# Stack rows element first, context and key/value weights loaded twice side by side, and a new order of DVE's work in a cross-attention and expert layer

## The chip, the cores and the metric

The kernel runs on one NeuronCore of a Trainium2 chip. The metric is the device time of one execution in microseconds (us), the median of several runs.

## What is computed

The input x is 8 sequences of 128 tokens with 256 features, the context 8 x 128 x 64. The reference, cut to what matters:

```python
# cross attention, 16 heads of 16 elements
qp = layernorm(x) @ Wq.T                       # 256 x 256
k, v = split(ctx @ Wkv_expand.T)               # Wkv_expand: 512 x 64
scores = einsum('bhqd,bhkd->bhqk', qh, kh) / 4, masked causally
out = softmax(scores) @ vh
x = x + out @ Wout.T
# experts: 8 of them, 2 chosen for each token
logits = xf @ (gate_weight + 2 * gate_B @ gate_A).T
gup = xf @ gate_up_proj[e] + lora;  h = silu(gates) * h
y = sum over the two chosen experts of weight * (h @ down[e] + lora)
x = x + y
```

All is float32, with tolerances that make the kernel split float32 values into parts that TensorE multiplies at speed.

## The kernel before, in words

The kernel is written with one instruction stream for each engine: SP (all DMA issues), POOL, ACT, DVE and TensorE (PE). Semaphores named in the code order them; within an engine everything runs in the order written, so one wait holds up everything behind it on that engine.

**Projections.** The batches form two groups of four (`GT = 4`). For each group DVE takes the statistics of x (`group_stats`, L552 and L553), POOL turns variances into 1/sqrt (`normaliser`, L301 and L302), DVE normalises into xhat (`normalise_group`, L557), TensorE transposes xhat (`x_T`, L867) and the context (`context_T`). The context and the key/value weights have 64 columns; their transposed blocks are wanted twice, in partitions 0 to 63 and 64 to 127 (the second copy is multiplied by the low part). `transpose_twice` (L840) makes the copies by a transposition (L842) and a plain product with the identity (L843). Then `kv_proj` and `q_proj` give k, v and q.

**Parts.** Scores are computed in bfloat16 from three parts of q and of k. ACT copies the first part from the bank (`first_part`), DVE subtracts it (`remainder`, L591), ACT makes the second part (`second_part`), and the third is a subtraction by POOL for k (`k_third_parts`, L296) and by DVE for q (`q_third_part`, L597). In POOL's stream `normaliser(0, GT, NT)`, which waits for the statistics of all eight batches, stands at L325, ahead of `k_third_parts(0)` at L327. SP writes the parts of a group to DRAM (`write_parts`, L225), the k set and then the q set, each set in three issues.

**Stacks.** For each batch b, `load_stack(b)` (L228 to L240) reads six stacked blocks of 16 rows back, in three loads for k_st and three for q_st, by `SLOTS = ((0, 0, 3), (1, 3, 2), (2, 5, 1))`: q part 0 three times against k parts 0, 1, 2; q part 1 twice against k parts 0, 1; q part 2 once against k part 0. A row is 16 heads x 128 tokens in bfloat16, 4 KB. One product over the 96 rows then gives all six part products of a head's scores (`s_chunk`, L976 and L980, a batch in four chunks). Both tensors have three buffers.

**Attention.** DVE takes the row maxima (`max_chunk`, L654) and splits them into three parts (`max_parts`, L669 to L673), TensorE transposes these (`max_T`, L1009), ACT copies them (`mT_copy`, L450) and SP loads them as three more rows of q_st (`load_max`, L244), so that the transposed scores (`sT_chunk`, L995) come out with the maximum subtracted. ACT takes the exponential (L456), POOL masks (L356), TensorE multiplies with v (L1168). Between the chunks TensorE, DVE, ACT and POOL also prepare the expert weights (`lora_product`, `merge`, `merge_high`, `merge_low`). The order of all of this is written out by hand in the loop over b from L1094 (TensorE) and L761 (DVE).

**SP's order** after the input loads: write k parts and q parts of group 0, `load_stack` of batches 0, 1, 2, `load_max(0)`, write k parts of group 1, `load_max(1)`, write q parts of group 1, then in turn `load_stack(3)`, `load_max(2)`, `load_stack(4)` and so on.

**Experts.** From about 111 us the expert products take over (L836 and L1060), 16 steps (two groups, eight experts).

Of the kernel before, what the change touches and what calls it, by code (L numbers as in the profile page):

```python
# [12 lines left out]
def cross_attention_moe_kernel(nc, x, ctx_kv, Wq, Wkv, Wout, gate_w, gate_A, gate_B,  # L13
# [11 lines left out]
    P = 128  # L25
    B, S, H = x.shape
    L = ctx_kv.shape[2]
    HD = 16
    NH = H // HD
# [3 lines left out]
    HC = H // P  # L33
    NT = B
    GT = 4
# [21 lines left out]
    ctx = ExitStack()  # L57
    with ctx:
        def sb(name, shape, dt=F32):
            return ctx.enter_context(nc.sbuf_tensor(name, shape, dt))  # L60
# [3 lines left out]


        x_sb = sb("x_sb", [P, NT, H])
        ctx_sb = sb("ctx_sb", [P, NT, L])
        raw = sb("raw", [P, HC * H + 4 * HC * L])
        wq_raw = raw[:, 0:HC * H].rearrange("p (c n) -> p c n", c=HC)
        wkv_raw = raw[:, HC * H:HC * H + 2 * HC * L].rearrange("p (c l) -> p c l", c=2 * HC)  # L70
        wo_raw = sb("wo_raw", [P, HC, H])
        gw_raw = sb("gw_raw", [E, H])
        ga_raw = sb("ga_raw", [R, H])
# [32 lines left out]
        ident = sb("ident", [P, P])  # L106
# [51 lines left out]
        qk_dram = nc.dram_tensor("qk_parts", (2, NT, 3, HD, NH // HC, HC, P), BF16, kind="Internal").ap()  # L158
# [27 lines left out]
        def S_(name):  # L186
            if name not in made:
                made[name] = sem(name)
            return made[name]
# [10 lines left out]
        @block.sync  # L200
        def _(sp):
            sp.dma_start(x_sb[:, 0:GT, :], x_v[:, 0:GT, :]).then_inc(ld["x0"], 16)
            sp.dma_start(wkv_raw, wkv_v).then_inc(ld["wkv"], 16)
            sp.dma_start(ctx_sb[:, :, :], ctx_v).then_inc(ld["ctx"], 16)
            sp.dma_start(wq_raw, Wq.rearrange("(c p) h -> p c h", p=P)).then_inc(ld["wq"], 16)
            sp.dma_start(x_sb[:, GT:NT, :], x_v[:, GT:NT, :]).then_inc(ld["x1"], 16)
            sp.dma_start(upA_raw[:, :], gup_A.rearrange("e r h -> (e r) h")).then_inc(ld["upA"], 16)
# [20 lines left out]
            def load_stack(b):  # L228
                if b >= 3:
                    sp.wait_ge(S_("sT_ready"), NC * (b - 2))  # L230
                sp.wait_ge(S_("k_written"), 16 * 3 * (b // GT + 1))
                for _, first, count in SLOTS:
                    src = qk_dram[1, b, 0:count].rearrange("s d h c n -> (s d) (h c n)")
                    dst = k_st[first * HD:(first + count) * HD, b % 3, :, :].rearrange("p h n -> p (h n)")
                    sp.dma_start(dst, src).then_inc(stack_loaded[b % 3], 16)  # L235
                sp.wait_ge(S_("q_written"), 16 * 3 * (b // GT + 1))
                for part, first, count in SLOTS:
                    src = qk_dram[0, b, part].rearrange("d h c n -> d (h c n)")[None].to_broadcast([count, HD, NH * P])
                    dst = q_st[first * HD:(first + count) * HD, b % 3, :, :].rearrange("p h n -> p (h n)")
                    sp.dma_start(dst, src).then_inc(stack_loaded[b % 3], 16)  # L240

# [297 lines left out]
        def _(dve):  # L539
# [20 lines left out]
            def normalise_group(g):  # L560
                dve.wait_ge(S_("rstd1_ready"), g + 1)
                if g:
                    dve.wait_ge(S_("x_T"), HC * g)
                for t in range(GT):
                    normalise(0, g * GT + t, xhat[:, t, :], "xhat_ready")
# [4 lines left out]
            def group_stats(g):  # L570
                dve.wait_ge(ld[f"x{g}"], 16)
                for t in range(g * GT, (g + 1) * GT):
                    norm_stats(0, t, "mv1_ready")
# [21 lines left out]
            def q_third_part(g, i):  # L595
                dve.wait_ge(S_("part2"), 4 * g + i + 1)
                dve.tensor_tensor(QK_PART(ORDER[i], 2), rest[:, i, :].rearrange("p (t n) -> p t n", t=GT),  # L597
                                  QK_PART(ORDER[i], 1), ALU.subtract).then_inc(S_("q_part3"), 1)
# [26 lines left out]
                        bank[2][:, ic * H + a * P:ic * H + (a + 1) * P].rearrange("p (h d) -> p h d", d=HD),  # L625
                        wqT_hi[:, ic, cols].rearrange("p (d h) -> p h d", d=HD), "wq_lo_ready", SCALE)
            input_lows(0)
            group_stats(1)
            remainder(0, 0)
            remainder(0, 1)  # L630
            normalise_group(1)
            remainder(0, 2)
            remainder(0, 3)
            q_third_part(0, 2)
            q_third_part(0, 3)
            dve.wait_ge(S_("lora_T"), 1)
            dve.tensor_scalar(loraBT[:, :, :].rearrange("p a n -> p (a n)"), bank[3][:, :], LORA, None, ALU.mult)\
                .then_inc(S_("lora_ready"), 1)
# [193 lines left out]
        def _(pe):  # L832
# [4 lines left out]
                if done:  # L837
                    last.then_inc(S_(done), 1)

            def transpose_twice(out_, in_):  # L840

                pe.transpose(out_[0:L, :], in_, ident[:, :])  # L842
                return pe.matmul(out_[L:P, :], in_, ident[:, :], start=True, stop=True)  # L843

            pe.wait_ge(S_("ident_made"), 1)

            pe.wait_ge(ld["wkv"], 16)
            for oc in range(2 * HC):
                last = transpose_twice(bank[3][:, oc * P:(oc + 1) * P], wkv_raw[:, oc, :])
            last.then_inc(S_("wkv_T"), 1)  # L850

            def context_T(g):
                if g == 0:
                    pe.wait_ge(ld["ctx"], 16)
                else:
                    pe.wait_ge(S_("v_ready"), 2 * g)
                for t in range(GT):
                    last = transpose_twice(bank[4][:, t * P:(t + 1) * P], ctx_sb[:, g * GT + t, :])
                last.then_inc(S_("c_T"), 1)

            def x_T(g):
# [351 lines left out]
```

## Time and profile before

| | us |
|---|---|
| median of 3 runs (206.45 to 208.89) | 207.55 |
| span of the profiled execution | 204.6 |
| TensorE busy | 166.9 (82%) |
| DVE busy | 132.7 (65%) |
| ACT busy | 79.9 (39%) |
| POOL busy | 60.0 (29%) |
| hardware DMA queue, share of 16 engines | 34.4% |

The profiled execution has a span, from its first to its last instruction, and no separate time; the span is 2.95 us under the median of the runs shown. The busy times overlap. A row of the timeline names the start, the time taken and the engine of a run of equal instructions; in brackets stand the idle time before it and what ended it. The granted clock is that of TensorE, 1.00 is 2.4 GHz and 0.50 is 1.2 GHz. A DMA share is the mean busy share of the core's 16 DMA engines.

### The profile page before, as it was taken

The page shows a single profiled execution, that of the slowest core. Times are in us where ns is not written, and L with a number is a line of the kernel's source. Part 1 is how long each engine was busy: PE and PEld are TensorE (multiplying, and loading weights), DVE is VectorE, ACT ScalarE, POOL GpSimd, SP SyncE. Part 2 cuts the span into 40 slices and gives each one's busy share as a digit, 9 for nine tenths or more (in the row PEclk, how much of TensorE's full clock was granted, in tenths as well). Part 3 has the DMA queues.
Part 4 walks back from the last instruction along what each step waited for, and adds up shares of the span by engine and source line. Part 5 has one row for each costly group of instructions (what it writes and reads, how often), then busy time and mean ns, then how long its engine had stood idle before and what let it go on. Part 6 is the DMA issues. An engine that isn't in the chain of part 4 may idle for free.

```text
span 204.6 us, 3326 instructions
## 1 busy us (share of the span) xinstructions
PE 166.9 (82%) x1238; PEld 131.4 (64%) x1245; DVE 132.7 (65%) x273; ACT 79.9 (39%) x151; POOL 60.0 (29%) x87
## 2 busy tenths in 40 slices
PE   0999297976888048887695979989999999999993
PEld 0458155854566037765574757778888888888882
DVE  3399955465887137888897878469639746545452
ACT  2136423750285014453553355742434623322230
POOL 7651900130055403764858383311000000000000
PEclk9999855799699757999999999999999999999999
DMA  6989466641618610314230000083000047300003
GB/s 170 232 215 386 139 179 167 157 120 61 186 33 222 133 68 33 84 69 123 58 112 32 3 4 0 26 245 145 0 3 0 0 164 254 103 0 0 5 0 103
DMA packets 23073, 20.63 MB, mean 101 GB/s; under 512 B 7400, under 2 KB 19456, under 8 KB 23056
## 3 DMA queue, kind: packets, MB, share of 16 engines
q1 hardware_dynamic: 23056, 20.41, 34.4%
q8 instruction: 10, 0.16, 0.3%
q14 instruction: 7, 0.06, 0.1%
HBM read 16.08 MB, written 4.23 MB: 99 GB/s over the span
## 4 chain that ended last, share of the span: by engine, by line
PE 42%; DMA 25%; DVE 18%; SPq 7%; ACT 3%; issue 3%; POOL 1%; DVEq 0%; ACTq 0%
PE bank L836 24%; DMA q_st<-qk_parts 17%; PE bank L1060 10%; DVE xhat L557 4%; DMA qk_parts<-parts 3%; SPq L240 3%; DMA q_st<-mT 2%; DVE m_sb L654 2%; DMA raw<-in_L_xattn_Wkv_expand 2%; SPq L235 2%; PE bank L980 1%; DVE stats L552 1%; PE bank L843 1%; SPq L244 1%; PE bank L867 1%
## 5 line engine op out<-in xcount | busy, mean ns | idle before, releaser
L654 DVE TENSOR_REDUCE m_sb<-bank 128x4 f32<-128x512 f32 x32 | 21.1, 681 | 14.0 <-PE bank L980 13.9
L356 POOL TENSOR_SCALAR_AFFINE_SELECT probsT<-probsT 128x512 f32<-128x512 f32 x32 | 20.1, 647 | 22.4 <-ACT probsT L456 22.4
L836 PE MATMUL bank<-xT_hi,up_hi 128*128 128x512 f32 x64 | 25.6, 400 | 0.0
L836 PE MATMUL bank<-xT_hi,up_lo 128*128 128x512 f32 x64 | 25.4, 397 | 0.0
L836 PE MATMUL bank<-xT_lo,up_hi 128*128 128x512 f32 x64 | 25.1, 393 | 0.0
L456 ACT ACTIVATE probsT<-bank 128x512 f32<-128x512 f32 x32 | 17.9, 590 | 17.9 <-PE bank L995 17.9
L980 PE MATMUL bank<-k_st,q_st 96*128 96x128 bf16 x128 | 13.8, 235 | 12.7 <-DMA q_st<-qk_parts 12.6
L378 ACT ACTIVATE h_hi<-up_w 128x512 fp32r<-128x512 f32 x16 | 10.1, 632 | 30.7 <-DVE up_w L726 26.1
L719 DVE TENSOR_TENSOR up_w<-bank,up_w 128x512 f32<-128x512 f32 x16 | 11.0, 688 | 14.2 <-PE bank L836 13.0
L1060 PE MATMUL bank<-dn_hi,h_hi 128*128 128x256 f32 x64 | 18.3, 285 | 0.1
L1060 PE MATMUL bank<-dn_lo,h_hi 128*128 128x256 f32 x64 | 18.2, 284 | 0.0
L1060 PE MATMUL bank<-dn_hi,h_lo 128*128 128x256 f32 x64 | 17.8, 279 | 0.0
L660 DVE TENSOR_TENSOR h_lo<-up_w,h_hi 128x512 fp32r<-128x512 f32 x16 | 11.0, 690 | 9.0 <-ACT h_hi L378 9.0
L976 PEld LDWEIGHTS bank<-causal,ident_b 128*128 128x128 bf16 x32 | 3.4, 105 | 18.2 <-DMA q_st<-qk_parts 13.8
L980 PEld LDWEIGHTS bank<-k_st,q_st 96*128 96x128 bf16 x128 | 11.1, 107 | 5.4 <-issue 1.9
L301 POOL TENSOR_SCALAR var_eps<-mv 128x1 f32<-128x1 f32 (+1 forms) x10 | 2.2, 224 | 41.4 <-DVE mv L553 41.4
L836 PEld LDWEIGHTS bank<-xT_hi,up_lo 128*128 128x128 f32 x64 | 12.0, 187 | 2.8
L976 PE MATMUL bank<-causal,ident_b 128*128 128x512 bf16 x25 | 10.9, 436 | 3.2 <-DMA q_st<-qk_parts 1.9
L836 PEld LDWEIGHTS bank<-xT_hi,up_hi 128*128 128x128 f32 x64 | 12.1, 188 | 2.1 <-issue 0.2
L836 PEld LDWEIGHTS bank<-xT_lo,up_hi 128*128 128x128 f32 x64 | 12.0, 188 | 2.1
L1060 PEld LDWEIGHTS bank<-dn_hi,h_hi 128*128 128x128 f32 x64 | 12.0, 188 | 1.0 <-DVE h_lo L660 0.3
L1060 PEld LDWEIGHTS bank<-dn_lo,h_hi 128*128 128x128 f32 x64 | 12.1, 188 | 0.4
(157 smaller groups left out, 377.9 us busy)
## 6 DMA issues: line engine op xcount, KB each, us to landing
probsT<-weights SPq DMA_DIRECT2D x16, 256.0 KB, 5.2
qk_parts<-parts SPq DMA_DIRECT2D x12, 256.0 KB, 3.0
up_w<-in_L_ffn_gate_up_proj SPq DMA_DIRECT2D x2, 1024.0 KB, 6.2
k_st<-qk_parts SPq DMA_DIRECT2D x8, 192.0 KB
q_st<-qk_parts SPq DMA_DIRECT2D x8, 192.0 KB
x_sb<-in_x SPq DMA_DIRECT2D x2, 512.0 KB, 4.7
dn_w<-in_L_ffn_down_proj SPq DMA_DIRECT2D x1, 1024.0 KB, 9.5
k_st<-qk_parts SPq DMA_DIRECT2D x8, 128.0 KB
```

The source lines that it names most:

```text
L240: sp.dma_start(dst, src).then_inc(stack_loaded[b % 3], 16)
L356: pool.affine_select(out=ch, in_=ch, compare_op=ALU.is_ge, fill=0.0, base=0, pattern=[[0, 4], [1, P]], channel_multiplier=-1).then_inc(S_( ...
L378: act.activation(out_, in_, ACT.Copy, scale=scale).then_inc(S_(done), 1)
L456: act.activation(probsT[:, b % 2, 4 * c:4 * c + 4, :].rearrange("p h n -> p (h n)"), bank[2 + c % 2][:, :], ACT.Exp).then_inc(S_("exp_done ...
L557: dve.tensor_scalar(out_, x_sb[:, t, :], mv[:, which, t, 0:1], rstd[:, which, t:t + 1], ALU.subtract, ALU.mult).then_inc(S_(done), 1)
L654: dve.reduce_max(m_sb[:, b % 2, 4 * c:4 * c + 4], bank[c % 2][:, :].rearrange("p (h n) -> p h n", h=4), AX.X)\
L660: dve.tensor_tensor(h_lo[:, k, :], h_f[:, k, :], h_hi[:, k, :].bitcast(F32), ALU.subtract)\
L719: dve.tensor_tensor(gated[:, k, :], bank[2 + k][:, :], silu[:, k, :], ALU.mult).then_inc(S_("gated_ready"), 1)
L836: last = pe.matmul(out_, a, m, start=start and i == 0, stop=stop and i == len(pairs) - 1, **kw)
L976: pe.matmul(bank[c % 2][:, :], ident_b[:, :], causal[:, :, :].rearrange("p h n -> p (h n)"), start=True, stop=True, skip_group_check=True)
L980: last = pe.matmul(bank[c % 2][:, j * P:(j + 1) * P], q_st[0:KS, b % 3, h, :], k_st[0:KS, b % 3, h, :], start=False, stop=True, skip_group ...
L1060: last = pe.matmul(bank[6 + t // 2][:, (t % 2) * H:(t % 2 + 1) * H], a[:, k, tok], w[:, e, :], start=e == 0 and t % 2 == 0 and i == 0, sto ...
```

## The change

Three edits. First, in `load_stack` the source of each load is read with the element (16 of them) as the outermost dimension and the part, or the copy, inside it; the rows of the stacks are then ordered by element and not by part, for k_st and q_st alike, and the sums over the rows are the same. Second, the key/value weights and the context are each loaded twice into neighbouring columns, and one transposition of a 128-wide block takes the place of the transposition and the product; their waits are for two loads. Third, DVE does group 0's remainders and q third parts before group 1's statistics and norms. POOL's, ACT's and the rest of SP's order stay.

```diff
-        ctx_sb = sb("ctx_sb", [P, NT, L])
+        ctx_sb = sb("ctx_sb", [P, NT, 2, L])
...
-            sp.dma_start(wkv_raw, wkv_v).then_inc(ld["wkv"], 16)
-            sp.dma_start(ctx_sb[:, :, :], ctx_v).then_inc(ld["ctx"], 16)
+            for k in range(2):
+                sp.dma_start(wkv_raw[:, :, k, :], wkv_v).then_inc(ld["wkv"], 16)
+            for k in range(2):
+                sp.dma_start(ctx_sb[:, :, k, :], ctx_v).then_inc(ld["ctx"], 16)
...
                 for _, first, count in SLOTS:
-                    src = qk_dram[1, b, 0:count].rearrange("s d h c n -> (s d) (h c n)")
+                    src = qk_dram[1, b, 0:count].rearrange("s d h c n -> d s (h c n)")
...
                 for part, first, count in SLOTS:
-                    src = qk_dram[0, b, part].rearrange("d h c n -> d (h c n)")[None].to_broadcast([count, HD, NH * P])
+                    src = qk_dram[0, b, part].rearrange("d h c n -> d (h c n)")[:, None, :].to_broadcast([HD, count, NH * P])
...
             input_lows(0)
-            group_stats(1)
             remainder(0, 0)
             remainder(0, 1)
-            normalise_group(1)
             remainder(0, 2)
             remainder(0, 3)
             q_third_part(0, 2)
             q_third_part(0, 3)
+            group_stats(1)
+            normalise_group(1)
...
-            def transpose_twice(out_, in_):
-                pe.transpose(out_[0:L, :], in_, ident[:, :])
-                return pe.matmul(out_[L:P, :], in_, ident[:, :], start=True, stop=True)
+            def transpose_doubled(out_, in_):
+                return pe.transpose(out_, in_.rearrange("p k l -> p (k l)"), ident[:, :])
```

## Rows read from the trace of the kernel before

**Rows 1.** The page: the chain that ended last, shares of the span by line.

```profile
PE bank L836 24%; DMA q_st<-qk_parts 17%; PE bank L1060 10%; DVE xhat L557 4%; DMA qk_parts<-parts 3%; SPq L240 3%; DMA q_st<-mT 2%; DVE m_sb L654 2%; DMA raw<-in_L_xattn_Wkv_expand 2%; SPq L235 2%; PE bank L980 1%; DVE stats L552 1%; PE bank L843 1%; SPq L244 1%; PE bank L867 1%
```

**Rows 2.** The chain of waits in order of time: start us, us, what.

```profile
37.86 11.99 DMA q_st<-qk_parts
...
51.01 5.08 DMA q_st<-mT
...
61.14 3.39 DMA qk_parts<-parts
...
65.28 8.60 DMA q_st<-qk_parts
```

**Rows 3.** Windows: length, PE, PEld, DVE, ACT, POOL busy, clock, DMA share, GB/s.

```profile
4.00:6.00 2.00, 0.86 (x3) 0.42 (x3) 1.45 (x6) 0.00 (x0) 1.24 (x4) 1.00 1.15 261
...
32.00:34.00 2.00, 1.22 (x5) 0.81 (x5) 0.87 (x2) 1.40 (x3) 0.00 (x0) 0.50 0.88 227
...
46.00:48.00 2.00, 1.98 (x15) 1.27 (x13) 1.45 (x4) 0.00 (x0) 0.00 (x0) 1.00 0.18 74
48.00:50.00 2.00, 0.10 (x1) 0.11 (x2) 0.68 (x4) 0.00 (x0) 0.00 (x0) 1.00 0.13 53
...
68.00:70.00 2.00, 0.00 (x0) 0.00 (x0) 0.00 (x0) 0.00 (x0) 0.83 (x1) 0.68 0.98 168
```

**Rows 4.** Timeline of PE: first score products of batches 1 and 3 to 7.

```profile
49.90 0.39 PE L976 MATMUL bank<-causal,ident_b 128*128 128x512 bf16 x1 [1.92 <-DMA q_st<-qk_parts]
...
74.32 0.63 PE L980 MATMUL bank<-k_st,q_st 96*128 96x128 bf16 x4 [8.01 <-DMA q_st<-qk_parts]
...
83.90 0.39 PE L980 MATMUL bank<-k_st,q_st 96*128 96x128 bf16 x4
...
93.51 0.39 PE L980 MATMUL bank<-k_st,q_st 96*128 96x128 bf16 x4 [1.34 <-DMA q_st<-qk_parts]
...
102.10 0.39 PE L980 MATMUL bank<-k_st,q_st 96*128 96x128 bf16 x4 [0.68 <-DMA q_st<-qk_parts]
...
111.40 0.39 PE L980 MATMUL bank<-k_st,q_st 96*128 96x128 bf16 x4 [1.39 <-DMA q_st<-qk_parts]
```

**Rows 5.** Window at the start of batch 3, columns as in rows 3.

```profile
74.00:79.00 5.00, 4.68 (x26) 3.74 (x28) 2.95 (x6) 0.90 (x2) 0.00 (x0) 0.50 0.14 57
```

**Rows 6.** Timeline of PE, 8 to 10 us: last weight block, then Wq's transpositions.

```profile
8.02 0.42 PE L842 MATMUL bank<-ident,raw 128*64 128x128 f32 x1
...
8.37 0.69 PE L843 MATMUL bank<-ident,raw 128*64 128x128 f32 x2
...
8.99 1.11 PE L902 MATMUL bank<-ident,raw 128*128 128x128 f32 x4
```

**Rows 7.** The page: DMA issues, KB each, median us from issue to landing.

```profile
out<-x_sb SPq DMA_DIRECT2D x4, 256.0 KB, 2.2
...
raw<-in_L_xattn_Wq SPq DMA_DIRECT2D x1, 256.0 KB, 5.0
```

**Rows 8.** Timeline of POOL and DVE, 19 to 29 us.

```profile
19.78 0.23 POOL L301 TENSOR_SCALAR var_eps<-mv 128x4 f32<-128x4 f32 x1 [6.72 <-DVE mv L553]
...
21.18 4.63 DVE L557 TENSOR_SCALAR xhat<-x_sb,mv,rstd 128x256 f32<-128x256 f32 x4 [0.32 <-POOL rstd L302]
21.29 2.47 POOL L296 TENSOR_TENSOR parts<-rest,parts 128x512 bf16<-128x512 f32 x2
...
27.11 1.29 DVE L597 TENSOR_TENSOR parts<-rest,parts 128x512 bf16<-128x512 f32 x2
```

**Rows 9.** Timeline of SP: both writes of group 0, first query stack.

```profile
23.79 6.14 SPq L225 DMA_DIRECT2D qk_parts<-parts  x6
...
32.99 1.99 SPq L240 DMA_DIRECT2D q_st<-qk_parts  x3
```

**Rows 10.** Timeline of DVE: first maxima of batch 0, group 1's q third parts.

```profile
44.85 1.29 DVE L654 TENSOR_REDUCE m_sb<-bank 128x4 f32<-128x512 f32 x2 [0.28 <-PE bank L980]
...
58.32 1.34 DVE L597 TENSOR_TENSOR parts<-rest,parts 128x512 bf16<-128x512 f32 x2
```

More of the change, by code:

```diff
@@ L66, in cross_attention_moe_kernel @@
         x_sb = sb("x_sb", [P, NT, H])
-        ctx_sb = sb("ctx_sb", [P, NT, L])
+        ctx_sb = sb("ctx_sb", [P, NT, 2, L])
         raw = sb("raw", [P, HC * H + 4 * HC * L])
         wq_raw = raw[:, 0:HC * H].rearrange("p (c n) -> p c n", c=HC)
-        wkv_raw = raw[:, HC * H:HC * H + 2 * HC * L].rearrange("p (c l) -> p c l", c=2 * HC)
+        wkv_raw = raw[:, HC * H:HC * H + 4 * HC * L].rearrange("p (c k l) -> p c k l", c=2 * HC, k=2)
         wo_raw = sb("wo_raw", [P, HC, H])
@@ L838, in products @@
                     last.then_inc(S_(done), 1)
-            def transpose_twice(out_, in_):
-                pe.transpose(out_[0:L, :], in_, ident[:, :])
-                return pe.matmul(out_[L:P, :], in_, ident[:, :], start=True, stop=True)
+            def transpose_doubled(out_, in_):
+                return pe.transpose(out_, in_.rearrange("p k l -> p (k l)"), ident[:, :])
             pe.wait_ge(S_("ident_made"), 1)
-            pe.wait_ge(ld["wkv"], 16)
+            pe.wait_ge(ld["wkv"], 32)
             for oc in range(2 * HC):
-                last = transpose_twice(bank[3][:, oc * P:(oc + 1) * P], wkv_raw[:, oc, :])
+                last = transpose_doubled(bank[3][:, oc * P:(oc + 1) * P], wkv_raw[:, oc, :, :])
             last.then_inc(S_("wkv_T"), 1)
@@ L853, in context_T @@
                 if g == 0:
-                    pe.wait_ge(ld["ctx"], 16)
+                    pe.wait_ge(ld["ctx"], 32)
                 else:
@@ L857, in context_T @@
                 for t in range(GT):
-                    last = transpose_twice(bank[4][:, t * P:(t + 1) * P], ctx_sb[:, g * GT + t, :])
+                    last = transpose_doubled(bank[4][:, t * P:(t + 1) * P], ctx_sb[:, g * GT + t, :, :])
                 last.then_inc(S_("c_T"), 1)
```

## The prediction

> **What bounds the kernel now.** I read the chain of waits first, by line, then the same chain in order of time. TensorE's long products are 24% and 10% of it; the one DMA edge that stands out is the load of the query stack, 17% of the span [rows 1]. In order of time it is 11.99 us before 49.9 and 8.60 us before 73.9, and the small load of the maxima (12 KB) takes 5.08 us where it follows those loads [rows 2]. The tail from about 111 us on is TensorE work back to back and no part of the change touches it, so whatever is won before 111 us arrives at the end whole.
>
> The windows say why the query loads are slow. In 48 to 50 us nothing else runs, and DMA has a share of 0.13 at 53 GB/s; in 46 to 48 it is 0.18 at 74 GB/s [rows 3]. Sixteen engines share the count, so these are two and three engines busy, 26.5 GB/s each. The stack is three loads per tensor, with 3, 2 and 1 copies. The query's source has the copies as its outermost dimension; three copies run on three engines, two on two. The key's source is (part, element), one run of 48, 32 or 16 rows, and while it moves (32 to 34 us, with other traffic) the share is 0.88 at 227 GB/s, 16.1 GB/s an engine. So in each query stack engine 0 carries 16 rows of 4 KB twice, and its part of the single copy: 135 KB, 5.1 us at 26.5 GB/s, which gives 15.3 us for the first three stacks.
>
> TensorE's rows show what waits: 1.92 us at 49.9, 8.01 at 74.32, then 1.34, 0.68 and 1.39 at three of the next four batches [rows 4]. The batch interval without such waits is 8.27 (83.90 to 93.51 less 1.34), 7.91 and 7.91. The interval 74.32 to 83.90 is 9.58: its start runs at a granted clock of 0.50 (1.2 GHz) until 79, after the 8 us in which TensorE stood still [rows 4, 5].
>
> **The change, part by part. 1: element first.** Both tensors' sources become (element, part) with 16 outermost. The bytes, the 4 KB rows and the three issues per tensor stay. From the rows I infer that the width follows the outermost count, so the query loads use 16 engines. The Trainium skill, DMA: Bandwidth & Descriptors, Why a DMA increments its semaphore by 16 and not by 1, says that the engine count is the largest number up to 16 that divides the slowest dimension of both sides; the widths 3 and 2 agree with it, and that 16 outermost gives 16 is shown by no row. The 384 KB of a query stack then take 1.5 us at the key loads' 16.1 GB/s an engine. The bounds: 0.9 us (26.5 GB/s), and 2.3 us (68 to 70 us, share 0.98 at 168 GB/s, 10.7 an engine [rows 3]). The row of the key loads is nearest. The Trainium skill, SBUF — State Buffer, Door 1: The DMA port swizzle, speaks against full width: rows 0 to 47 or 48 to 79 reach 8 ports, rows 80 to 95 only 4, at 27.2 GB/s a port. An estimate from that page is 2.1 us for the 384 KB; by it the sum would be at most 0.6 us worse.
>
> **2: transposes.** A 64-wide block takes a transposition (0.42) and a two-pass product (0.69), 0.97 us from one block to the next; a 128-wide transposition takes 1.11 / 4 = 0.28 [rows 6]. Four blocks each for weights and either context group: 3.9 becomes 1.1, so 2.8 us less, three times. The price is 384 KB more in 256-byte rows, 1.5 us at the 261 GB/s of the window at 4 us [rows 3], and two more issues at 0.5. The weights land 0.5 later (5.14 to 5.65) and their transposition ends at 6.75 instead of 9.06. Wq lands at 2.37 + 5.0 = 7.4 now [rows 7] and at 8.9 then; TensorE takes it at 8.99 now, so that gain stops there: Wq's transposition still ends near 10.0. Then context 0 ends at 11.1, x_T(0) at 13.1 and the projections start at 13.2 instead of 16.24 (DVE's xhat for group 0 runs ahead of POOL's long spread then, and is not late). 3.0 us earlier. The later loads land 1.5 us later, all well before use: the expert weights are first read at 36.
>
> **3: DVE's order.** Between DVE's input lows and its last q third part of group 0 now stand statistics (2.1 us, their end at 19.7 releases POOL's 19.78 row) and norms (21.18 to 25.8, after POOL's rstd) [rows 8]. Without them, from DVE's input lows ending at 14.5 (17.5 less 3.0) and with ACT's steps as long as now (0.6 a step): two remainders to 16.4, ACT's v copies and second parts to 17.9, its first parts to 19.2, remainders to 19.9, second parts 20.5, third parts 21.2. Instead of 28.4 [rows 8]: 7.2 us earlier.
>
> This gain is not used, and here is the new wait. POOL's queue holds group 1's rstd **ahead** of group 0's k third parts. Statistics now run 21.2 to 23.3, so POOL's rstd comes 3.65 us later (19.78 to 23.4), its third parts end at 27.4 instead of 23.76, and SP writes k before q [rows 8, 9]. Six issues of 0.5: k 27.4 to 29.0, q to 30.6 with the last at 30.1; a set lands about 3.4 us after its last issue [rows 2], 1.0 us more behind the k set that is still moving: 34.5, where the first query stack's issue stands at 32.99 now [rows 9]. Every stack's issue shifts by 1.5 us. Norms of group 1 end at 29.4 instead of 25.8, x_T(1) at 31.5; the shorter context transposition gives back 2.8 of this 3.65, and the later path (lora weights, group 1's projections) is 1.1 late. I add 0.3 for clock: TensorE stands still longer before x_T(1), and the clock stands at 0.50 at 32 to 34 already [rows 3], and until 38. If it lasted through q_proj(1), 12 products of 0.24 would take 0.43: 2.3 us, the upper bound.
>
> **Sum along the path.** q_proj(1) ends near 44.6; DVE's last remainder near 46.0 (44.56 now), so batch 0's maxima and their parts (44.85 to 48.8 now [rows 10]) end at 49.35: only 0.6 later, since TensorE's two score chunks are waiting for DVE instead of the reverse. Stack 1 has long landed: batch 1's scores start at 48.6, not 49.9. The mT load is issued at 50.0 and needs 2.0 instead of 5.08 (a 256 KB store on all engines needs 2.2 [rows 7]): 52.0 instead of 56.09. DVE: eight maxima and merges of 0.62 from 49.35, max_parts 0.85, merge(5) 0.65, q third parts of group 1 1.34, end 57.1 instead of 59.66 [rows 10]. SP issues the q writes at 57.1 to 58.7; with 3.39 us from the last issue they land at 61.6 instead of 64.5 [rows 2]. Query stack 3: issues 1.9, then 1.8 to land: 65.3 instead of 73.88. TensorE is done with batch 1 at 63.8 (its transposition of batch 2's maxima comes 4.9 us after DVE's third parts as now, 62.0; then 1.7 of products), so it waits 1.5 us and starts batch 3's scores at 65.7 instead of 74.32: **8.6 us**. With a wait this short the clock should stay at 1.00: 9.58 becomes 8.1, **1.5 us**. Batches 5 to 7 lose 1.34 + 0.68 + 1.39 = **3.4 us**, since a stack issued by 86.5 lands by 89 and is read at 92.2. Together 13.5 us.
>
> The span is 204.6, the median of three runs 207.55; I take the 2.95 around the span as fixed. 204.6 - 13.5 + 2.95 = **194.0 us**.
>
> **Rivals.** (a) The wide loads get in each other's way at 10.7 GB/s an engine: key and query 2.3 us each. Stack 3 lands 1.7 us later, TensorE stands still 3.3 us and starts at clock 0.50 as at 74 us: 1.5 more. 197.2 us. For: the window at 68 us. Against: that window mixes with the narrow loads. (b) The first stage is worse: clock 0.50 through q_proj(1), and DVE's whole chain with it, 2.0 us; stack 3 hides nothing of it. 196.0 us. (c) The first stage does better: stack 3's wait vanishes (1.5) and q third parts come 1 us sooner. 191.5 us. (d) Slower: the loads stay on three and two engines, because the width does not follow the source's outermost dimension. Then POOL's wait decides: it holds k's third parts and so every stack by 1.5 us, the path 37.86 to 49.85 takes it whole, and group 1's writes and stack 3 behind it. 209.1 us, and 210.6 if the clock also falls once more there. It decides as soon as the wide loads save less than 1.5 us on stacks 1 and 3.
>
> **How the numbers follow.** The forecast 0.55, (a) 0.15, (b) 0.12, (c) 0.1, (d) 0.08. The range takes (a) to (c) and the bounds of the load rate: 190.5 to 199. Differences under 1% can't be told from none. Faster 0.92; of (d), half lies within 1% and half beyond: same 0.04, slower 0.04.
>
> **What would show it.** DMA share over 0.5 while only a query stack loads, no window at 0.13; POOL's rstd for group 1 near 23 to 25 us and SP's k writes near 27 with the q parts done at 21; mT's first load at 2 us; the wait before batch 3 at 1 to 3 us; none at batches 5 to 7; intervals of 8. Wrong would be: waits for query stacks at batches 5 to 7, a clock of 0.50 in 65 to 79 us, or new waits for POOL or DVE that fill the intervals to their old length.

## The result, and the profile after

| | before | after |
|---|---|---|
| median, us | 207.0 (4 runs, 205.62 to 208.89) | 195.45 (4 runs, 193.12 to 195.85) |
| ratio to before, with its interval | | 0.942 [0.932, 0.952] |
| profiled execution: span | 204.6 | 193.6 |
| profiled execution: its own time | not given | 195.37 |

The change makes the kernel 5.8% faster; 194.0 was predicted. Every ratio here leaves the longer, disturbed executions of a kernel out; the profiled executions of stacks_undone, transposes_only and dve_order_undone are of that kind, so their rows are read for order and waits, not for sums.

The page of the kernel after: TensorE's granted clock in 40 slices (tenths), the hardware DMA queue (packets, MB, share of 16 engines), and the chain that ended last by line (answers to [rows 1]).

```profile
PEclk9999955899999999999999999999999999999998
...
q1 hardware_dynamic: 24840, 20.81, 38.4%
...
PE bank L838 32%; PE bank L1060 10%; DVE m_sb L656 8%; DVE xhat L559 2%; DMA raw<-in_L_xattn_Wq 2%; DMA q_st<-qk_parts 2%; DVE up_w L610 2%; DVE stats L554 2%; PE bank L1113 2%; DMA qk_parts<-parts 2%; DVE m_parts L674 2%; DVE m_parts L675 1%; DVE dn_w L610 1%; DVE xT_lo L550 1%; DVE parts L599 1%
```

The query stacks fall from 17% of the chain to 2%, DVE's row maxima rise from 2% to 8%. The granted clock is low once, in slices 6 to 8, and then not again before the last slice, at the end of the program; before it was low in four more slices (the 11th and the 14th to 16th).

The timeline of TensorE in the kernel after (start, us, what; idle time before it and what ended it): group 1's transposition, and the first product of batches 0, 1, 3, 4 and 7 (answers to [rows 4]).

```profile
31.46 1.97 PE L867 MATMUL bank<-ident,xhat 128*128 128x128 f32 x8 [11.05 <-DVE xhat L559]
...
44.47 0.39 PE L976 MATMUL bank<-causal,ident_b 128*128 128x512 bf16 x1
...
48.61 0.38 PE L976 MATMUL bank<-causal,ident_b 128*128 128x512 bf16 x1
...
67.03 0.39 PE L976 MATMUL bank<-causal,ident_b 128*128 128x512 bf16 x1 [2.22 <-DMA q_st<-qk_parts]
...
75.02 0.38 PE L976 MATMUL bank<-causal,ident_b 128*128 128x512 bf16 x1
...
99.88 0.38 PE L976 MATMUL bank<-causal,ident_b 128*128 128x512 bf16 x1
```

One wait for a query stack is left of the six (five stand in [rows 4], the sixth was 1.22 us at 44.43, batch 0): 2.22 us at batch 3. The intervals are 8.0 us from batch 3 to 4, then 24.86 for the next three together. The trace of before, like most here, has no record of the L976 product that opens a batch at most of these places; its L980 row starts 0.2 us later at the full clock, and a wait read there is longer by as much. From batch 7's first score product to the end the kernel takes as long as before: 204.6 - 111.40 = 93.2, and 193.6 - 100.09 = 93.5 (its L980 row stands 0.21 behind the L976 row above).

Windows of the kernel after, columns as in [rows 3]:

```profile
46.00:48.00 2.00, 1.81 (x15) 0.99 (x14) 1.89 (x4) 1.15 (x2) 0.00 (x0) 1.00 0.68 199
48.00:50.00 2.00, 1.65 (x12) 1.02 (x11) 1.86 (x7) 0.18 (x1) 0.00 (x0) 1.00 0.01 4
```

The third stack's loads move at 199 GB/s, beside TensorE's work; in the same stretch before 74 and 53 GB/s stood [rows 3]. From 48 to 50 us DMA is empty.

The timeline of DVE, POOL and SP in the kernel after, 21 to 37 us: group 0's last q third parts, then group 1's norms (answers to [rows 8, 9]).

```profile
21.68 1.47 DVE L599 TENSOR_TENSOR parts<-rest,parts 128x512 bf16<-128x512 f32 x2
...
25.38 0.23 POOL L303 TENSOR_SCALAR var_eps<-mv 128x4 f32<-128x4 f32 x1 [11.04 <-DVE mv L555]
...
26.78 4.63 DVE L559 TENSOR_SCALAR xhat<-x_sb,mv,rstd 128x256 f32<-128x256 f32 x4 [1.49 <-POOL rstd L304]
26.89 2.47 POOL L298 TENSOR_TENSOR parts<-rest,parts 128x512 bf16<-128x512 f32 x2
...
36.81 1.80 SPq L242 DMA_DIRECT2D q_st<-qk_parts  x3
```

POOL has been waiting 11.04 us for the statistics, and TensorE 11.05 us for the norms. In the kernel before TensorE's wait at this place was 4.14 us.

### The profile page after: what moved, and what is told of

Its sections match the earlier page's. It is cut to its first block, busy times and chain, and to the rows that moved or that the text cites. A ratio compares the mean times of both kernels' runs of the same rounds, so it can differ in the third digit from the quotient of the medians.

```text
span 193.6 us, 3287 instructions
## 1 busy us (share of the span) xinstructions
PE 155.0 (80%) x1221; PEld 126.1 (65%) x1221; DVE 132.1 (68%) x273; ACT 80.1 (41%) x151; POOL 60.0 (31%) x87
## 2 busy tenths in 40 slices
DMA packets 24857, 21.03 MB, mean 109 GB/s; under 512 B 9184, under 2 KB 21240, under 8 KB 24840
## 3 DMA queue, kind: packets, MB, share of 16 engines
q1 hardware_dynamic: 24840, 20.81, 38.4%
## 4 chain that ended last, share of the span: by engine, by line
PE 51%; DVE 33%; DMA 6%; SPq 2%; issue 2%; ACT 2%; POOL 1%; DVEq 0%; POOLq 0%; ACTq 0%
PE bank L838 32%; PE bank L1060 10%; DVE m_sb L656 8%; DVE xhat L559 2%; DMA raw<-in_L_xattn_Wq 2%; DMA q_st<-qk_parts 2%; DVE up_w L610 2%; DVE stats L554 2%; PE bank L1113 2%; DMA qk_parts<-parts 2%; DVE m_parts L674 2%; DVE m_parts L675 1%; DVE dn_w L610 1%; DVE xT_lo L550 1%; DVE parts L599 1%
## 5 line engine op out<-in xcount | busy, mean ns | idle before, releaser
L976 PE MATMUL bank<-causal,ident_b 128*128 128x512 bf16 x32 | 12.3, 385 | 5.4 <-DVE m_sb L656 3.0
L867 PE MATMUL bank<-ident,xhat 128*128 128x128 f32 x16 | 3.9, 426 | 11.1 <-DVE xhat L559 11.1
L980 PEld LDWEIGHTS bank<-k_st,q_st 96*128 96x128 bf16 x128 | 9.9, 97 | 4.2
L980 PE MATMUL bank<-k_st,q_st 96*128 96x128 bf16 x128 | 12.4, 219 | 0.0
```

The costliest lines, as they stand in the source:

```text
L867: last = pe.transpose(bank[ic][:, t * P:(t + 1) * P], xhat[:, t, ic * P:(ic + 1) * P], ident[:, :])
L976: pe.matmul(bank[c % 2][:, :], ident_b[:, :], causal[:, :, :].rearrange("p h n -> p (h n)"), start=True, stop=True, skip_group_check=True)
L980: last = pe.matmul(bank[c % 2][:, j * P:(j + 1) * P], q_st[0:KS, b % 3, h, :], k_st[0:KS, b % 3, h, :], start=False, stop=True, skip_group ...
```

## The experiments

Parts alone and parts undone come first, then the two waits under dispute.

**stacks_only**: the kernel before with the first edit alone.

```diff
-src = qk_dram[1, b, 0:count].rearrange("s d h c n -> (s d) (h c n)")
+src = qk_dram[1, b, 0:count].rearrange("s d h c n -> d s (h c n)")
...
-src = qk_dram[0, b, part].rearrange("d h c n -> d (h c n)")[None].to_broadcast([count, HD, NH * P])
+src = qk_dram[0, b, part].rearrange("d h c n -> d (h c n)")[:, None, :].to_broadcast([HD, count, NH * P])
```

> The kernel before with the element-first stacks alone. My theory: the width of the query loads is the whole gain, and the other two parts add nothing to it. Stage one stays as before, so batch 0's scores start near 43.3 and batch 3's near 66.4; no clock drop, intervals of 8.0 to 8.3. Time within 1 us of the changed kernel's 195.4, rather under it: 194.9. Rival: the shorter transpositions (2.8 us three times) carry part of the gain themselves; then this kernel is 198 or slower.

Measured: 193.17 us, ratio 0.936 [0.931, 0.940]. This edit alone gives more than the whole change. The queue's line of the page, then TensorE's wait at batch 3, in stacks_only:

```profile
q1 hardware_dynamic: 23272, 20.41, 36.3%
```

```profile
65.87 0.39 PE L980 MATMUL bank<-k_st,q_st 96*128 96x128 bf16 x4 [2.05 <-DMA q_st<-qk_parts]
```

The packet count shows the width itself. The kernel before has 23056; here it is 216 more, 27 for each of 8 batches, with the same bytes in the same rows. (16 - 3) + (16 - 2) is 27: one small packet more for each engine that joins the loads with three and two copies. The Trainium skill, DMA: Bandwidth & Descriptors, Why a DMA increments its semaphore by 16 and not by 1, says that each engine that takes part ends with a write of +1 to the semaphore, and that there are as many as the largest number up to 16 that divides the slowest dimension of both sides; the count agrees with both.

**stacks_undone**: the kernel after with the old `load_stack`, the same lines reversed.

```diff
-    src = qk_dram[0, b, part]...[:, None, :].to_broadcast([HD, count, NH * P])
+    src = qk_dram[0, b, part]...[None].to_broadcast([count, HD, NH * P])
```

> The changed kernel with the stacks read part first as before; transpositions and DVE's order stay changed. My theory: the narrow loads bound the middle again, and POOL's wait puts the first query stack 3.8 us later (36.8 in the changed kernel against 33.0), which the chain through stack 1 and stack 3 takes whole: 210.8 us, slower than before. Rival 1: the two other parts have a gain of their own (2.8 us or more): 204 or less. Rival 2: the stage has slack and the delay is swallowed: 207.

Measured: 210.54 us, ratio 1.017 [1.009, 1.025]; 24624 packets, 216 fewer than after. Without the wide loads the rest of the change is a loss of 1.7%; rival (d) had 209.1, or 210.6 with one more fall of the clock. Timeline of TensorE and SP, then a window, columns as in [rows 3], of stacks_undone:

```profile
29.47 1.97 PE L867 MATMUL bank<-ident,xhat 128*128 128x128 f32 x8 [11.05 <-DVE xhat L559]
34.81 1.97 SPq L242 DMA_DIRECT2D q_st<-qk_parts  x3
46.10 0.39 PE L980 MATMUL bank<-k_st,q_st 96*128 96x128 bf16 x4 [3.28 <-DMA q_st<-qk_parts]
51.77 0.39 PE L976 MATMUL bank<-causal,ident_b 128*128 128x512 bf16 x1 [2.12 <-DMA q_st<-qk_parts]
76.98 0.63 PE L980 MATMUL bank<-k_st,q_st 96*128 96x128 bf16 x4 [7.17 <-DMA q_st<-qk_parts]
```

```profile
50.00:52.00 2.00, 0.23 (x2) 0.11 (x3) 0.39 (x3) 0.00 (x0) 0.00 (x0) 1.00 0.13 53
```

The old waits are back, and so is the window of two engines. The first query stack is issued at 34.81, 1.8 us later than before [rows 9], and TensorE waits 3.28 us for it: with narrow loads the late stacks come last, and not the norms.

**load_per_copy**: the kernel before, rows still part first, but one load of 16 rows for each copy (TensorE's wait for a stack then counts nine loads instead of six).

```diff
 for part, first, count in SLOTS:
-    src = qk_dram[0, b, part]...[None].to_broadcast([count, HD, NH * P])
-    dst = q_st[first * HD:(first + count) * HD, b % 3, :, :]...
+    for copy in range(first, first + count):
+        src = qk_dram[0, b, part].rearrange("d h c n -> d (h c n)")
+        dst = q_st[copy * HD:(copy + 1) * HD, b % 3, :, :]...
```

> The kernel before, with each copy of a query part loaded by a load of its own, 16 rows with the element outermost, still part first in the stack: six query loads instead of three. It tells the width of a load from the order of the rows. Width theory: these loads are wide too, so the narrow stretches (share 0.13) are gone; the price is three more issues of 0.6 us for each stack, so batch 3's scores start near 68.5 and the time is 197.5 us, 196 to 199.5. Rival, the order of rows or of reads is what counts: as before, 205 to 209.

Measured: 193.81 us, ratio 0.936 [0.929, 0.943], the same as stacks_only; 23656 packets, 600 more than before, which is 8 x (6 x 16 - 21). So the width is the cause and the order of the rows is not. I was 3.7 us too dear. 1.7 of it is the base: I had put stacks_only at 194.9, and it measured 193.17. About 1.0 is the issues, three more of them taken at 1.8 us where they cost 0.8: this stack's six take 0.44 each, later stacks' up to 0.53 (SP of load_per_copy). The last 1.0 us I can't place.

```profile
32.98 2.62 SPq L241 DMA_DIRECT2D q_st<-qk_parts  x6
```

**width8**: the kernel after, the query's element dimension written as 8 x 2.

```diff
-.rearrange("d h c n -> d (h c n)")[:, None, :].to_broadcast([HD, count, NH * P])
+.rearrange("(x y) h c n -> x y (h c n)", x=8)[:, :, None, :].to_broadcast([8, HD // 8, count, NH * P])
```

> The changed kernel with the element of the query loads written as 8 x 2, so that the outermost dimension is 8: the same rows in the same places. It gives the width a third value. Theory (the outermost count is the width): query loads run on 8 engines, their stretches show shares near 0.5, a query stack takes 3 us on each of its engines instead of 5 or 1.5; stack 3 lands 1 to 1.5 us later and TensorE's wait before it is 3.3 to 3.7 instead of 2.2 us: 197 us, 195.5 to 199. Rival: adjoining dimensions are merged to 16 before the split: as the changed kernel, 194 to 196, and a wait of 2.2.

Measured: 194.81 us, ratio 0.942 [0.935, 0.949], 24840 packets like the kernel after; 8 engines would have left 24 fewer for each batch. The width stayed 16, as the rival put down for it has it (adjoining dimensions are merged before the split; the packets show the width, not the reason). It says nothing on the price of 8 engines. But its trace is a second look at batch 3 with the same loads:

```profile
67.50 0.39 PE L980 MATMUL bank<-k_st,q_st 96*128 96x128 bf16 x4 [2.93 <-DMA q_st<-qk_parts]
```

The wait ends 0.25 us later than in the kernel after (67.25 for this product), and here the granted clock falls to 0.50 from 70 to 72 us. In the kernel after it stayed at 1.00.

**halves**: the kernel after, each query load cut by element into two loads with 8 outermost.

```diff
+for half in range(2):
+    src = qk_dram[0, b, part, half * 8:half * 8 + 8].rearrange("d h c n -> d (h c n)")[:, None, :]\
+        .to_broadcast([8, count, NH * P])
+    row = first * HD + half * 8 * count
```

> The changed kernel with each query load cut in two by element, 8 outermost in each: the same rows in the same places, six loads a stack (as many issues as with a load for each copy), each on 8 engines if the outermost count sets the width. Engine 0 then carries 12 rows of 4 KB a stack instead of 6, and engines 8 to 15 none. Theory: stretches in which a query stack moves show shares near 0.5 and 100 to 140 GB/s; stack 3 lands 1 to 1.5 us later (issues 2.7 instead of 1.8 us, then 0.5 more), TensorE waits 3.3 to 3.7 us before it instead of 2.2, and the time is 196.8 us, 195.5 to 198. Rival (the width is something else than the outermost count): shares as in the changed kernel, a wait of 2.2 to 2.6 and 194 to 196 us.

Measured: 195.71 us, ratio 0.945 [0.934, 0.955]; 24840 packets, since 6 x 8 is 3 x 16, so each half did run on 8 engines (on 16 it would be 48 packets more for each batch). A window of halves, columns as in [rows 3], and TensorE's wait at batch 3:

```profile
43.00:45.00 2.00, 1.99 (x15) 1.29 (x14) 1.29 (x3) 1.56 (x3) 0.00 (x0) 1.00 0.42 121
```

```profile
66.61 0.61 PE L979 MATMUL bank<-causal,ident_b 128*128 128x512 bf16 x1 [3.96 <-DMA q_st<-qk_parts]
```

The transfers run at 0.42 of 16 engines, between the narrow loads and the wide. The wait at batch 3 is 3.96 us instead of 2.22, and the first products behind it take 0.61 us, at a granted clock of 0.50 in 66 to 70 us; yet the time can't be told from the kernel after. Part of the reason is that this execution's first stage ran 1.6 us earlier (first parts written at 27.74, not 29.38), as shown further down; its span is still 1.3 us longer, 194.9.

**transposes_only**: the kernel before with the second edit alone.

```diff
+for k in range(2):
+    sp.dma_start(wkv_raw[:, :, k, :], wkv_v).then_inc(ld["wkv"], 16)
...
+def transpose_doubled(out_, in_):
+    return pe.transpose(out_, in_.rearrange("p k l -> p (k l)"), ident[:, :])
```

> The kernel before with the doubled loads and single transpositions alone. Theory: group 0's parts are written 2.7 us earlier (the first query stack is issued at 30.3, as in the kernel with DVE's old order), and the narrow loads carry this through: 204 us where the kernel before has 206 to 208, a ratio of 0.987. Rival: the longer loads eat it: no change.

Measured: 206.8 us in the median of ten runs, ratio 0.985 [0.980, 0.990]. The median of the kernel before, run beside them, is 206.8 too, so whether this edit alone gives 1.5% or nothing is open.

Timeline of TensorE in transposes_only:

```profile
22.95 1.10 PE L867 MATMUL bank<-ident,xhat 128*128 128x128 f32 x8 [2.92 <-DVE xhat L559]
41.52 0.63 PE L980 MATMUL bank<-k_st,q_st 96*128 96x128 bf16 x4 [5.27 <-DMA q_st<-qk_parts]
...
71.23 0.63 PE L980 MATMUL bank<-k_st,q_st 96*128 96x128 bf16 x4 [7.95 <-DMA q_st<-qk_parts]
```

x_T(1) comes 2.9 us earlier than in the kernel before (25.87), but TensorE then waits for the narrow query loads all the same, 5.27 and 7.95 us, and starts at the lower clock behind each (0.63 us for a row that takes 0.39).

**dve_order_only** and **dve_order_undone**: the third edit alone on the kernel before, and the kernel after without it.

```diff
+group_stats(1)
 remainder(0, 0)
 remainder(0, 1)
+normalise_group(1)
 remainder(0, 2)
 remainder(0, 3)
 q_third_part(0, 2)
 q_third_part(0, 3)
-group_stats(1)
-normalise_group(1)
```

The lines are those of dve_order_undone; dve_order_only has them the other way round.

> The kernel before with DVE's new order alone. My theory: group 1's statistics move behind group 0's q third parts, POOL's rstd and the k third parts behind them follow, and the first query stack is issued about 5 us later (38 instead of 33); the narrow loads are in the chain, so the time is 211.5 us, 210 to 213. Rival: the earlier q parts help the writes, and the time stays 206 or falls.

> The changed kernel with DVE's old order: group 1's statistics ahead of group 0's remainders, its norms between them. My theory: in the changed kernel group 1's statistics, POOL's rstd, xhat and x_T(1) are the chain in 23 to 33 us, so the new order costs time. With the old order, x_T(1) starts near 22 to 23 instead of 31.5, q parts of group 0 end near 25, batch 0's scores start near 36 instead of 44.5, and nothing later takes it back: 187 us, 185.5 to 190. Rival: the stack loads need group 0's parts as early as they are now, and TensorE waits for them instead: 194 to 196.

Measured: dve_order_only 213.18 us, ratio 1.034 [1.023, 1.046]; dve_order_undone 188.62 us, ratio 0.906 [0.899, 0.912], 7 us under the kernel after. Timeline of DVE, POOL and TensorE in dve_order_undone:

```profile
17.03 0.23 POOL L303 TENSOR_SCALAR var_eps<-mv 128x4 f32<-128x4 f32 x1 [2.08 <-DVE mv L555]
...
18.43 4.63 DVE L559 TENSOR_SCALAR xhat<-x_sb,mv,rstd 128x256 f32<-128x256 f32 x4 [0.32 <-POOL rstd L304]
...
23.11 1.97 PE L867 MATMUL bank<-ident,xhat 128*128 128x128 f32 x8 [4.57 <-DVE xhat L559]
```

Group 1's rstd starts at 17.03 instead of 25.38, its transposition at 23.11 instead of 31.46: the same 8.35 us. About 2 us of these are chance: stacks_undone, with the same order as the kernel after, has the two at 23.38 and 29.47 (last section). The third edit is a loss in both surroundings, by 3.4% and by 3.6%.

**pool_k_first**: the kernel after, POOL's k third parts of group 0 ahead of group 1's rstd.

```diff
+k_third_parts(0)
 normaliser(0, GT, NT, "mv1_ready", NT)
 pool.memset(v_sb[:, :, :, HD:VW], 1.0).then_inc(S_("v_ones"), 1)
-k_third_parts(0)
```

> The changed kernel with POOL's order changed too: the k third parts of group 0 ahead of the wait for group 1's statistics. Theory A (norms): what the new DVE order costs is that group 1's statistics, rstd, xhat and x_T(1) come late; the parts of group 0 and their stacks are not what TensorE waits for. Then SP's writes start near 21 instead of 29 and the time hardly follows: only xhat, which no longer runs beside the k third parts, ends 2 us earlier: 193.5 us. Theory B (the wait that I put on record): POOL's wait in front of the k parts holds back the gain of the early q parts. Then the time falls by 4 us or more, to 191 or less.

Measured: 193.73 us, ratio 0.939 [0.930, 0.948], against 0.942 for the kernel after. Timeline of pool_k_first:

```profile
17.29 2.29 POOL L298 TENSOR_TENSOR parts<-rest,parts 128x512 bf16<-128x512 f32 x2 [2.33 <-ACT parts L380]
...
19.61 5.74 SPq L227 DMA_DIRECT2D qk_parts<-parts  x6
...
25.17 2.96 DVE L559 TENSOR_SCALAR xhat<-x_sb,mv,rstd 128x256 f32<-128x256 f32 x4 [1.49 <-POOL rstd L304]
...
28.19 1.97 PE L867 MATMUL bank<-ident,xhat 128*128 128x128 f32 x8 [9.39 <-DVE xhat L559]
29.33 1.80 SPq L242 DMA_DIRECT2D q_st<-qk_parts  x3
```

Group 0's parts are written 9.8 us earlier and its first query stack is issued 7.5 us earlier, and the end moves by 1.9 us (span 191.7). Those stacks had been in time without it: in the kernel after TensorE does not wait at batch 0's first product (44.47), nearly 6 us behind the last issue of that stack (38.61). What gain there is goes with x_T(1), 3.3 us earlier: 1.7 because the norms have less of POOL beside them (2.96 us instead of 4.63), and 1.6 because this execution's first stage was among the early ones, which is chance. The clock also came back later here, at 36.6 us instead of 35.2, which hides part of it.

**spread_later**: dve_order_undone, with POOL's spread of the down lora weights behind group 1's k third parts.

```diff
-pool.tensor_tensor(dnA_bd, dnA_raw[...], expert_rows[...], ALU.mult).then_inc(S_("dnA_spread"), 1)
 k_third_parts(1)
+pool.tensor_tensor(dnA_bd, dnA_raw[...], expert_rows[...], ALU.mult).then_inc(S_("dnA_spread"), 1)
```

> DVE's old order, with the wide stacks and the doubled transposition, and one thing more: POOL's spread of dnA (1.94 us, beside which one xhat takes 1.98) moves behind the k third parts of group 1. xhat of group 1 then ends 1.6 to 2.0 us earlier, and it is in the chain: 1.7 us less than the kernel with the old order alone, 186.7 against 188.6. Rival: clock or stack 3 take it back: the same within 0.5 us.

Measured: 185.55 us, ratio 0.898 [0.890, 0.906].

Timeline of DVE and TensorE in spread_later:

```profile
18.07 3.08 DVE L559 TENSOR_SCALAR xhat<-x_sb,mv,rstd 128x256 f32<-128x256 f32 x4 [0.32 <-POOL rstd L304]
...
21.21 1.10 PE L867 MATMUL bank<-ident,xhat 128*128 128x128 f32 x8 [0.87 <-DVE xhat L559]
```

The norms take 3.08 us instead of 4.63, as expected. The ratio is 0.8 points under dve_order_undone's, about 1.6 us where 1.9 was expected, but the two intervals overlap. TensorE's wait is 0.87 us instead of 4.57; half of that difference is the norms' earlier end (21.15, not 23.06), the other half that this execution's projections ended 1.8 us later. Its eight transpositions take 1.10 us and not 1.97, and no slice of the page but the last has a clock under 9 tenths.

**thirds_early**: spread_later, with group 1's q third parts on DVE behind batch 1's first maximum, and SP's write of them right behind the k parts.

```diff
 max_chunk(1, 0)
+q_third_part(1, 2)
+q_third_part(1, 3)
 merge(1)
...
 merge(5)
-q_third_part(1, 2)
-q_third_part(1, 3)
...
 load_max(0)
 write_parts(1, 1)
+write_parts(1, 0)
 for b in range(NT):
     if b + 1 < NT:
         load_max(b + 1)
-    if b == 0:
-        write_parts(1, 0)
```

> As the one before, and group 1's q third parts move on DVE from behind merge(5) to behind batch 1's first maximum, and SP writes them right behind the k parts, ahead of the load of batch 1's maxima. My theory: stack 3 is the last place where TensorE waits for a query stack (2.2 to 2.5 us and a clock of 0.50 after it); its parts would be written 5 us earlier, so the wait is gone, for 1.3 us of DVE in the chain before it: 2 to 2.5 us less, 184.5. Rival: DVE and SP are in the chain themselves here, mT(1) comes 1.6 us later, and nothing is won: 186.5 or more.

Measured: **182.64 us**, ratio 0.883 [0.874, 0.892]. The wait at batch 3 shrinks from spread_later's 2.63 us to 0.50. Timeline of TensorE in thirds_early, batches 0 and 3:

```profile
34.33 0.39 PE L979 MATMUL bank<-k_st,q_st 96*128 96x128 bf16 x4 [1.57 <-DMA q_st<-qk_parts]
...
55.02 0.39 PE L979 MATMUL bank<-k_st,q_st 96*128 96x128 bf16 x4 [0.50 <-DMA q_st<-qk_parts]
```

This is the fastest of all, 6 points under the kernel after (0.883 against 0.942, intervals apart), and 2.9 us under spread_later, run beside it (182.06 to 183.01 against 184.62 to 186.47); 2 to 2.5 were expected. Batch 3 was not the last place with such a wait: TensorE waits 1.57 us for batch 0's stack, as it did 1.25 us in spread_later. Group 0's stacks, which nobody waits for in the kernel after, are waited for once the norms come early.

## Why the prediction came out

**The account.** In ratios to the kernel before, edit by edit: stacks 0.936; with the transposes 0.906; with DVE's order 0.942. So the three edits are -6.4%, -3.0% and +3.6%. Alone on the kernel before they are -6.4%, -1.5% and +3.4%. The two small ones are less sure than the large one: the median of all four runs of dve_order_undone stands at 0.914 of the kernel before, by which they would be -2.2% and +2.8%, and the transposes alone may be nothing. That they are worth more where no narrow query load stands behind them is likely and not shown. The sum did count the third edit as a loss of time for group 1 ("x_T(1) at 31.5", its end; it ended at 33.43, and at 31.44 in stacks_undone), but never said that leaving it out would be 7 us better. That 194.0 came within 1.5 us is in part luck: two errors of the sum go opposite ways, as shown below.

**1, element first: right.** The wide loads remove the waits, as predicted, and the width comes from the outermost count (stacks_only, load_per_copy, stacks_undone, packets). The rate of a stack alone can't be read: the loads of neighbouring tensors overlap. The estimate from the Trainium skill, SBUF — State Buffer, Door 1: The DMA port swizzle (2.1 us and not 1.5 for a stack) is therefore neither borne out nor refuted.

**2, transposes: right.** The weights' transposition, then the projections' first product:

```profile
5.83 1.09 PE L843 MATMUL bank<-ident,raw 128*128 128x128 f32 x4 [5.83 <-DMA raw<-in_L_xattn_Wkv_expand]
...
8.82 1.12 PE L902 MATMUL bank<-ident,raw 128*128 128x128 f32 x4 [1.90 <-DMA raw<-in_L_xattn_Wq]
...
13.26 0.76 PE L838 MATMUL bank<-cT,wkv_hi 128*128 128x512 f32 x1 [0.72 <-DVE cT L550]
```

Predicted were 5.65, 8.9 and 13.2. As foreseen, the gain on the weights ends in the wait for Wq, and the context's is kept. That is right for the times; what they are worth at the end is the open question above.

**3, DVE's order: times right, cause wrong.** q third parts ended at 23.1 (predicted 21.2), rstd came at 25.38 (23.4), k's write at 29.38 (27.4), the first query stack at 36.81 (34.5): all about 2 us late by one cause, the first rise of TensorE's clock (last section). In stacks_undone, where it rose early, the four stand at 21.16, 23.38, 27.39 and 34.81, as predicted. The step "This gain is not used, and here is the new wait. POOL's queue holds group 1's rstd ahead of group 0's k third parts" is refuted for the wide loads by pool_k_first: with that wait gone the stacks come 7.5 us earlier and the ratio stays within its interval. The gain is not used because nobody waits for group 0's stacks there; what the edit costs comes through group 1's statistics and norms, whose chain the page shows (starts, us, the chain of waits of the kernel after):

```profile
23.16 0.35 DVE stats L554
...
25.70 1.06 POOL rstd L304
26.78 4.64 DVE xhat L559 x4
31.46 1.97 PE bank L867 x8
```

**From 31 to 50 us: right**, but by luck. x_T(1) ended at 33.43 and not at 31.5. The clock was back at 1.00 from 35.2 on, where I had put it low until 38, so that group 1's projections made up what the late norms had lost. In stacks_undone, where x_T(1) did end at 31.4, they ended at 42.8, 1.8 us before the forecast: the clock's low stretch was put too long by nearly as much as the first rise cost. So q_proj(1) ends at 44.6 (44.6), batch 0's parts of maxima at 49.4 (49.35), batch 1's scores start at 48.61 (48.6), the first load of maxima is issued at 50.12 (50.0), and batch 0's transposed scores start at 52.89 without a wait for it, instead of 56.13.

**Batch 3: mis-sized by 1.3 us.** TensorE starts at 67.03 and not at 65.7. DVE's part of it, in the timeline of DVE and POOL of the kernel after:

```profile
54.04 1.22 POOL L358 TENSOR_SCALAR_AFFINE_SELECT probsT<-probsT 128x512 f32<-128x512 f32 x2 [9.84 <-ACT probsT L458]
54.13 0.57 DVE L671 TENSOR_SCALAR m_parts<-m_sb 128x16 bf16<-128x16 f32 x1
54.74 0.55 DVE L672 SCALAR_TENSOR_TENSOR m_rest<-m_sb,m_parts 128x16 f32<-128x16 f32 x1
...
56.23 1.98 DVE L599 TENSOR_TENSOR parts<-rest,parts 128x512 bf16<-128x512 f32 x2
```

The earlier load of maxima brings POOL's masks of batch 0 on top of DVE's small splits: 0.57 and 0.55 us, where two like them (L674, L675) take 0.17 without POOL, and 1.98 for the q third parts instead of [rows 10]'s 1.34. They end at 58.2, 1.1 late. The Trainium skill, SBUF — State Buffer, SBUF: two separate sides, has DVE and GpSimd share one pair of ports, an exclusive lock held for a whole instruction, among others for DVE instructions with two SBUF inputs. These rows fit that: L671 and L672 end at 54.70 and 55.29, and the two masks at 54.68 and 55.26. Then the chain of waits of the kernel after:

```profile
59.19 3.34 DMA qk_parts<-parts
...
63.21 3.77 DMA q_st<-qk_parts
```

From the parts' landing (62.53) to the stack's it is 4.45 us, and I had 1.9 + 1.8: 0.75 late, which is the latency behind the last issue.

**Intervals of batches 4 to 7: mis-sized by 0.8 us.** I took 3.4 us of waits off; 83.90 to 111.40 was 27.50 and is 24.86 (75.02 to 99.88), 2.64 less. Subtracting a wait from an interval gave 7.91, but behind the wait stood the chain of maxima: TensorE now waits 0.43 us for DVE's m_sb in each batch (8% of the chain), and the interval is 8.3. The clock's term (9.58 becomes 8.1) came out, 7.99, but the step "With a wait this short the clock should stay at 1.00" held by luck: in the trace of width8 it fell to 0.50 behind a wait that ended 0.25 us later, and in dve_order_undone's behind one of 2.53 us, while pool_k_first's kept 1.00 behind 2.90.

**The sum.** 7.3 at batch 3, 1.6 of clock, 2.6 of intervals, less 0.2 because the rows at either end are different products, is 11.3 at batch 7; 11.0 at the end, with 13.5 predicted. So the sum took off 2.5 us too much. The term "2.95 around the span" put 1.15 too much back: profiled runs with both numbers have 1.8 (195.37 - 193.6, 193.9 - 192.2; 1.7 in 183.01 - 181.3). 2.95 was the distance from one execution to the median of others. The two errors leave the 1.4 between 194.0 and the result.

**Rivals.** (a) and (b) did not occur in the profiled execution: the wait at batch 3 was 2.22 us at clock 1.00, and the clock came back before q_proj(1). (c) would have needed the last wait to go. (d), that the loads stay narrow, is what stacks_undone builds: 1.017 of before. There the first query stack is issued at 34.81 and TensorE waits for it, as (d) has it. pool_k_first was not run with narrow loads, so what a new order of POOL would give back there stays open.

## What to carry to other kernels

Look at the DMA share while one load runs alone: 0.13 of 16 engines is two engines, and the source's outermost count is the first thing to change. Before a gain "not used" is put down to a wait, ask who waits for the result: TensorE's idle time before x_T(1), 4.14 us in the kernel before, named DVE's norms, and an order that finishes off the near consumer's work first delays the next group's only chain. A change that is a win as a whole is still worth taking apart; here one of its three edits cost about half of what the best one gave. And a number that comes out is no proof of its terms: here a late norm stage met a clock that came back early, and a sum that saved too much met a constant that was too large.

## What the runs showed of the hardware that was not expected

- **The first rise of the clock differs between executions.** Group 0's products (128x512) take 0.63 us, then 0.40. I read that as TensorE's clock, since the same two durations stand at granted clocks of 0.50 and 1.00 elsewhere (L979 in halves: 0.63 at 67.86 and 68.72, at 0.50, and 0.39 at 78.11, at 1.00). The kernel after and stacks_undone have the same work up to there:

```profile
17.67 0.63 PE L838 MATMUL bank<-xT_hi,wqT_lo 128*128 128x512 f32 x1
...
18.38 0.40 PE L838 MATMUL bank<-xT_lo,wqT_hi 128*128 128x512 f32 x1
```

```profile
13.82 0.39 PE L838 MATMUL bank<-cT,wkv_lo 128*128 128x512 f32 x1
```

The first are of the kernel after (rise at 18.1), the second of stacks_undone (before 13.8). The projections end at 20.4 and 18.4, and POOL's rstd stands at 25.38 and 23.38. The other kernels with the second edit fall into the same two camps: early in halves, pool_k_first, dve_order_undone and thirds_early, at 17.3 to 18.1 in width8, spread_later and transposes_only. So 2 us of the first stage are chance, and one profile can't settle a step of that size there. The page's column of the granted clock shows 1.00 in both, and only the durations tell it.
- **Issues.** Where SP does not wait, three loads with copies take it 0.6 us each (1.80 for three, 3.64 for six in halves), six of a single copy 0.44 to 0.53 each.
- **DVE beside POOL.** Four norms took 4.63 us with POOL's k third parts and its spread beside them, 2.96 with the spread alone (pool_k_first) and 3.08 with the third parts alone (spread_later). The chain that ends last holds them.
